# A graph network kernel: in each pass SP fetches some of the gathered rows, in place of the Pool's gather

## The reference

```python
h = relu(layernorm(x)); x = x + segment_sum(norm[:, None] * h[src], dst)      # norm from softmaxes of the edge weights
h = relu(layernorm(x)); for beta in betas (2): h = agnn_layer(h, src, dst, beta); x = x + h
h = relu(layernorm(x)); x = x + segment_sum(h[src] @ W16[type16], dst)        # 16 relations
h = relu(layernorm(x)); x = x + segment_sum(h[src] @ W32[type32], dst) / deg + h @ W_self + bias
```

## Time and profile before

| | |
|---|---|
| median of 3 runs | 12,770.65 us |
| profiled execution, its own time | 12,762.47 us |
| span of the profiled execution | 12,760.7 us |
| POOL busy | 9,421.5 us (74%) |
| PE busy | 7,159.6 us (56%) |
| DVE busy | 5,982.9 us (47%) |
| ACT busy | 2,502.0 us (20%) |
| granted TensorE clock | 0.503 of full speed |

### The profile page before, as it was taken

One profiled execution on the slowest core, in us unless ns is written; L12 is line 12 of the kernel. 1 busy time (PEld: TensorE's weight loads), 2 busy tenths in 40 slices (PEclk: granted clock), 3 DMA queues, 4 the chain that ended last, 5 costly groups with the idle time before them and its releaser, 6 DMA issues.

```text
span 12760.7 us, 121408 instructions
## 1 busy us (share of the span) xinstructions
PE 7159.6 (56%) x34866; PEld 5995.3 (47%) x34866; DVE 5982.9 (47%) x13186; ACT 2502.0 (20%) x5819; POOL 9421.5 (74%) x9933
## 2 busy tenths in 40 slices
PE   8430000444444688888878888875555554444444
PEld 2230000333333577777778888863333343333333
DVE  6991000333333587888778888862222222122221
ACT  0000000000000355555545555530000000000000
POOL 5777777777777677777767777767777776777777
PEclk5555555555555555555555555555555555555555
DMA  1001001111111222222222222232222222111112
GB/s 37 5 5 20 5 5 29 34 27 28 27 28 27 37 54 54 54 54 54 51 62 65 65 65 66 65 50 49 51 50 50 50 51 46 27 27 27 27 27 26
DMA packets 430148, 505.99 MB, mean 40 GB/s; under 512 B 235856, under 2 KB 245584, under 8 KB 417584
## 3 DMA queue, kind: packets, MB, share of 16 engines
q0 software_dynamic: 317504, 279.59, 14.5%
q1 hardware_dynamic: 97730, 214.09, 4.8%
q10 hardware_dynamic: 14316, 4.81, 0.2%
HBM read 397.49 MB, written 94.54 MB: 39 GB/s over the span
## 4 chain that ended last, share of the span: by engine, by line
POOL 68%; issue 23%; DVE 3%; PE 3%; DMA 2%; SPq 0%; DVEq 0%; ACT 0%; POOLq 0%; ACTq 0%
POOL Z L659 60%; POOL bins_dst L635 8%; DVE pd L1085 1%; DMA Z<-table,pd 1%; PE ps L1477 1%; PE ps L1479 1%; PE ps L1478 1%; DVE ps L1080 1%; PE ps L1558 0%; PE ps L1593 0%; DMA Z<-table_a,pd 0%; PE ps L1435 0%; PE ps L1524 0%; SPq L553 0%; DMA Z<-table_b,pd 0%
## 5 line engine op out<-in xcount | busy, mean ns | idle before, releaser
L659 POOL DMA_INDIRECT Z<-table,pd x4986 | 4704.8, 944 | 1623.0 <-issue 1513.6
L1575 PE MATMUL ps<-Z 128*128 128x65 f32 x9972 | 2326.7, 420 | 3334.5 <-DMA Z<-table_b,pd 1197.3
L1575 PEld LDWEIGHTS ps<-Z 128*128 128x128 f32 x9972 | 2186.3, 329 | 3654.2 <-issue 2348.2
L1131 DVE TENSOR_TENSOR Z<-ps,pd 128x768 f32<-128x768 f32 x831 | 795.0, 957 | 2836.8 <-PE ps L1575 2828.7
L635 POOL DMA_INDIRECT bins_dst<-slot_d x1612 | 1576.9, 978 | 589.7 <-issue 489.7
L659 POOL DMA_INDIRECT Z<-table_a,pd x1662 | 1568.3, 944 | 564.4 <-issue 560.6
L659 POOL DMA_INDIRECT Z<-table_b,pd x1662 | 1568.2, 944 | 545.0 <-issue 505.3
L1558 PE MATMUL ps<-Z 128*128 128x65 f32 x6648 | 1527.6, 417 | 268.8 <-DVE Z L1203 258.9
L1558 PEld LDWEIGHTS ps<-Z 128*128 128x128 f32 x6648 | 1467.2, 331 | 349.7 <-issue 216.9
L1524 PE MATMUL ps<-pay_d,hot 128*128 x6648 | 1554.8, 424 | 122.1 <-issue 97.4
L1524 PEld LDWEIGHTS ps<-pay_d,hot 128*128 128x128 f32 x6648 | 1463.7, 330 | 230.4 <-issue 227.8
(11 more groups left out here) (245 smaller groups left out, 8690.2 us busy)
## 6 DMA issues: line engine op xcount, KB each, us to landing
pay_d<-locals_ SPq DMA_DIRECT2D x92, 1152.0 KB
Z<-table,pd POOLq DMA_INDIRECT x4986, 2.4
table_b<-pay_d SPq DMA_DIRECT2D x192, 256.0 KB, 2.4
Z<-table_a,pd POOLq DMA_INDIRECT x1662, 2.4
Z<-table_b,pd POOLq DMA_INDIRECT x1662, 2.4
bins_dst<-slot_d POOLq DMA_INDIRECT x1612, 2.1
table_a<-kept SPq DMA_DIRECT2D x94, 256.0 KB
slot_d<-pay_d SPq DMA_DIRECT2D x62, 91.0 KB, 1.9
```

The source lines that it names most:

```text
L659: nc.gpsimd.indirect_dma_start(rows[:, at.slot, j, 0:width], None, ps_.table, bass.IndirectOffsetOnAxis(ap=pdi[:, g * ITEMS + j, ps_.colum ...
L1131: v.tensor_tensor(hot_d[:, at.three, :, :], every, nodes, ALU.is_equal).then_inc(hot_f_made, 1)
L1575: last = mm(p_pair[:, at.three, bass.ds(offset_of(at, j), ROW)], hot_d[:, at.three, j, :], given, start=False, stop=j == ITEMS - 1)
```

## The change

In five lists `TAKEN`, one for each pass, stand the groups 25, 37, 49, ... (in pass 2 from 30, in pass 3 from 28, in pass 4 from 21), every twelfth group up to 256: 20, 20, 19, 20 and 20 of them, 99 in all. Of these groups the Pool leaves out the last item, the sixth. SP fetches its 128 rows instead. It reads their numbers, which an own DMA has brought into `cand` or `node_max`, eight at a time into registers (one TENSOR_LOAD of 8 words), and issues for each row one DMA from the table to `fetched`, a new tensor in DRAM. 64 rows (`half_fetched`) stand behind the store of each block r = 0 to 39; behind the store of block r = 2t + 2 stands `into_ring`, which waits for the rows of the t-th fetched item and for the ring's place and moves them by one DMA into the ring. The consumers of these groups wait for this DMA as well (`ring_filled`). A row of 64 floats is split into 16 pieces of 4, a row of 65 floats (AGNN passes) into 13 pieces of 5. The chunks of `locals_` move ahead by one block.

```diff
+    FIRST = (25, 25, 30, 28, 21)
+    TAKEN = [range(first, NG - 20, 2 * RING) for first in FIRST]
+    fetched = scratch("fetched", (sum(len(t) for t in TAKEN), P, ROW))
...
+            def half_fetched(ps_, turn):
+                t, half = turn // 2, turn % 2
+                if t >= len(TAKEN[ps_.p]):
+                    return
...
+                for first in range(half * P // 2, (half + 1) * P // 2, BATCH):
+                    known = nc.values_load_multi_w_load_instructions(
+                        index_of[ps_.p % 2][t:t + 1, first:first + BATCH].bitcast(I32), engines=[sp.engine], min_val=0,
+                        max_val=ps_.table.shape[0] - 1, skip_runtime_bounds_check_because="rows of edges or the row of the padding")[1]
+                    for k in range(BATCH):
+                        sp.dma_start(fetched[n, first + k:first + k + 1, 0:width],
+                                     ps_.table[bass.ds(known[k], 1), :]).then_inc(row_fetched[n % 10], 16)
...
+            def into_ring(ps_, turn):
+                t = turn // 2 - 1
+                if turn % 2 or not 0 <= t < len(TAKEN[ps_.p]):
+                    return
...
+                sp.wait_ge(row_fetched[n % 10], (n // 10 + 1) * P * 16)
+                sp.wait_ge(msg_made if ps_.scaled else summed, done(at.g + (ps_.gather if ps_.scaled else ps_.every) - RING))
+                sp.dma_start(rows[:, at.slot, ITEMS - 1, 0:width], fetched[n, :, 0:width]).then_inc(ring_filled, 16)
...
             for r in range(NB):
                 store_rows(0, r)
+                into_ring(p_edge, r)
+                if r == 1:
+                    indices(p_agnn[0])
+                half_fetched(p_edge, r)
...
@@ gather @@
                         if j == ITEMS - 1 and ago:
-                            pool.wait_ge(gathered[ago.slot], (ps_.gathers(ago) + 1) * (16 * THREE))
+                            pool.wait_ge(gathered[ago.slot], landed(ps_, ago))
+                        if j == ITEMS - 1 and g in TAKEN[ps_.p]:
+                            continue
...
@@ multiply; the same in messages and sums_per_node @@
-                    dve.wait_ge(gathered[at.slot], (ps_.gathers(at) + 1) * (16 * THREE))
+                    dve.wait_ge(gathered[at.slot], landed(ps_, at))
+                    if at.g in TAKEN[ps_.p]:
+                        dve.wait_ge(ring_filled, ring_fills(ps_, at))
```

More of the change, by code:

```diff
@@ L357, in gnn_program @@
         local_loaded = [sem("local_loaded0"), sem("local_loaded1")]
+        indices_loaded = sem("indices_loaded")
+        row_fetched = [sem(f"row_fetched{k}") for k in range(10)]
+        ring_filled = sem("ring_filled")
         hot_t_made, hot_32_made, pen_made, fallen = sem("hot_t_made"), sem("hot_32_made"), sem("pen_made"), sem("fallen")
@@ L388, in gathers, with taken_before, landed, ring_fills @@
                 return self.nth * -(-(NG - at.slot) // RING) + at.rnd
+        def taken_before(ps_, at):
+            return sum(1 for q in range(ps_.p + 1) for g in TAKEN[q] if g % RING == at.slot and (q < ps_.p or g <= at.g))
+        def landed(ps_, at):
+            return (ps_.gathers(at) + 1) * (16 * THREE) - 16 * taken_before(ps_, at)
+        def ring_fills(ps_, at):
+            return 16 * (sum(len(TAKEN[q]) for q in range(ps_.p)) + TAKEN[ps_.p].index(at.g) + 1)
         p_edge = Pass(EDGE, 0, 0, 0, tables[0])
@@ new lines, in half_fetched @@
+            def half_fetched(ps_, turn):
+                t, half = turn // 2, turn % 2
+                if t >= len(TAKEN[ps_.p]):
+                    return
+                if turn == 0:
+                    sp.wait_ge(indices_loaded, 16 * (ps_.p + 1))
+                    if ps_.scaled:
+                        sp.wait_ge(table_stored, table_stores(ps_.p))
+                    else:
+                        for h in range(HALVES[ps_.p - 1]):
+                            sp.wait_ge(half_stored[h], 16 * NB * (ps_.p - 2 if h < HALVES[2] else 1) + 1)
+                n = sum(len(TAKEN[q]) for q in range(ps_.p)) + t
+                width = ROW if ps_.softmax else D
+                for first in range(half * P // 2, (half + 1) * P // 2, BATCH):
[5 more added lines that the diff above has]
+                                     ps_.table[bass.ds(known[k], 1), :]).then_inc(row_fetched[n % 10], 16)
@@ new lines, in into_ring @@
+            def into_ring(ps_, turn):
+                t = turn // 2 - 1
+                if turn % 2 or not 0 <= t < len(TAKEN[ps_.p]):
+                    return
+                at = At(TAKEN[ps_.p][t])
+                n = sum(len(TAKEN[q]) for q in range(ps_.p)) + t
+                width = ROW if ps_.softmax else D
+                sp.wait_ge(row_fetched[n % 10], (n // 10 + 1) * P * 16)
+                sp.wait_ge(msg_made if ps_.scaled else summed, done(at.g + (ps_.gather if ps_.scaled else ps_.every) - RING))
+                sp.dma_start(rows[:, at.slot, ITEMS - 1, 0:width], fetched[n, :, 0:width]).then_inc(ring_filled, 16)
@@ L575, in store_halves @@
                 for h in range(HALVES[p]):
+                    if h and chunk_between:
+                        chunk(*chunk_between)
                     sp.wait_ge(part_kept, part_of(p, rank, (h + 1) * 512 // WIDTH[p]))
@@ L591, in _ @@
                 store_rows(1, r)
[L592 to L597, removed]
+            for c in range(2, 4):
+                chunk(*chunk_of(2 * NG, c))
+            for r in range(NB):
+                store_halves(2, r, chunk_of(2 * NG, r + 4) if r + 4 < chunks else None)
+                into_ring(p_agnn[1], r)
+                if r == 1:
+                    indices(p_plain[0])
+                half_fetched(p_agnn[1], r)
             for r in range(NB):
                 store_halves(3, r)
+                into_ring(p_plain[0], r)
+                if r == 1:
+                    indices(p_plain[1])
+                half_fetched(p_plain[0], r)
             for r in range(NB):
@@ L1571, in sums_per_node @@
                         pe.wait_ge(half_gathered[at.slot], (ps_.gathers(at) + 1) * (16 * THREE))
-                        pe.wait_ge(gathered[at.slot], (ps_.gathers(at) + 1) * (16 * THREE))
+                        pe.wait_ge(gathered[at.slot], landed(ps_, at))
+                        if at.g in TAKEN[ps_.p]:
+                            pe.wait_ge(ring_filled, ring_fills(ps_, at))
                     for j in range(ITEMS):
```

32 lines of the change are left out of this document (26 added, 6 removed).

## The result

The changed kernel takes **15,573.83 us** (median of 4 runs, 15,567.83 to 15,581.91), the kernel before 12,771.22 us beside it (12,762.2 to 12,772.03): a ratio of 1.2194 with a 95% interval of 1.2179 to 1.221. The direction was forecast, the size was not: +2,803 us against +1,119, and outside the range.

The account below looks back on a forecast made before the run. The Pool's gathers bound the kernel; SP turns of 49.0 to 55.2 us, above 44.3, would add 1,126 us over the five passes, gathers saved included, to 12,762.5: 13,890 us on the median's scale, range 12,635 to 14,750.

Parts of the forecast that it names:

- the bound: All five passes: the Pool's gather sets the pace, 60% of the span, one start every 1.249 us.
- the saving: Pool: 99 gathers of 1.249 us removed, 123.6 us less; 12,647 us if all else keeps up.
- the mechanism: SP's queue: next store and fill wait behind 64 fetches, so too long turns delay the Pool; +1,126 us over five passes.
- the formula for a pass: Each pass: block 0's store plus 40 turns (38 in pass 2), landing and remaining gathers; pass 0 +115 us, pass 1 +348.
- Rows of 65 floats go out in 13 pieces.: SP's fetch in AGNN passes: 0.08 us more, 0.59 us each, 37.8 us for 64; bounds 0 and 0.11.
- Address and DMA 0.51 us.: SP's fetch of one row: 0.51 us with its address, 32.6 us for 64; bounds 0.43 to 0.66.
- Register loads of 8 words 1.8 us.: SP's row-number loads: 1.8 us each, eight with gaps 14.6 us a turn; other values 2.0, 1.2, lowest 0.27.
- The rule on increments: SP's DMAs on fewer than 16 engines: sequencer writes missing increments; if free, passes 1 and 2 lose some 400 us less.
- the fill in time: Ring, pass 0: with SP on time, a late fill costs no Pool time until some 44 us late.
- the DMA engines no limit: DMA engines: busy 17% to 26%; 12,672 more rows in small pieces add a few per cent.

Follow-up runs that it names:

- e14: Against the kernel before: the 99 items are neither gathered by the Pool nor fetched, their places keep old rows; 12,660.08 us, 0.9899.
- e9: Against the changed kernel: SP fetches each row as one piece into SBUF (unused columns of `iota`) and fills the ring from there; 12,635.74 us.
- e12: Against the changed kernel: SP still fetches all rows to DRAM, but the Pool gathers everything and nobody fills the ring; 15,281.06 us.
- e11: Against the changed kernel: AGNN passes fetch 80 floats in 16 pieces of 5 instead of 65 in 13; 13,950.81 us.
- e13: Against the changed kernel: 49 groups taken instead of 99, each fetched in four turns of 32 rows, still to DRAM; 12,693.45 us.
- e1: First run of the kernel that neither gathers nor fetches the 99 items, beside a slow kernel before; 15,578.67 against 15,699.22 us, 0.9917.
- e8: First run of the changed kernel with 49 groups, each fetched in four turns of 32 rows, beside a slow kernel before; 16,573.92 us, 1.0614.
- e5: First run of the changed kernel with empty SP loops in place of all fetches, the Pool gathering everything; 33,361.3 us, 2.1364.
- e10: Against the changed kernel: empty SP loops replace all fetches and their loads, the Pool gathers everything; 25,248.13 us, 1.9786.

## Why the prediction was right in its direction and wrong in its size

**Right: the bound, the saving, the mechanism.** The Pool's gathers were the bound and 99 of them are worth 124 us (e14: 130, e9: 126). SP can't leave a turn early, and the Pool's end follows SP's stores: the last gather starts 141 us after that of block 40 in pass 0 (4479.63 - 4338.26), where the working had 139 to the gather's end, and 158 in pass 1, where it had 152. So the formula for a pass holds, and nearly the whole error of 1,684 us (15,574 - 13,890) is in the turns put into it. One part was left out. The working named the fill as what frees the ring. The waits of DVE and ACT for the stores and chunks do nearly the same by themselves (e12), and the fill adds 290 us of 2,803.

**Wrong, and nearly three quarters of it: "Rows of 65 floats go out in 13 pieces."** The step took 0.08 us more for a fetch, with 0.11 as the upper bound from the two DMAs of L501. Measured: 0.758 instead of 0.492 us, +0.27, three times as much, and +0.5 us for each load behind it. That is 64 x 0.27 + 8 x 0.5 = 21 us a turn instead of 5. Turns of 54.7 and 55.2 us were forecast, 72.5 and 73.5 came. The forecast had put some 400 us on the 13 pieces; with them gone (e11) the kernel takes 13,951 us, 1,623 less. That is 1,220 of the 1,684 us. That 13,951 lies so near the 13,890 of the forecast is chance, for by the same working a kernel without the 13 pieces would take about 13,490; the other 460 us are the smaller errors below and in the rest of a turn. The bound failed because it rested on a single pair of DMAs from before the loops, which differ in rows as well as in pieces, and because a price for the instruction behind wasn't looked for.

**Wrong: "Address and DMA 0.51 us."** It was 0.675, beyond the upper bound of 0.66. The DMA alone took 0.492 and not 0.332. The nearest row by price was L517's 0.486, which I had kept only as an end of the range; I had reasoned by the number of engines, and the loads of x have that in common with a fetch too but cost a third less. 64 x 0.165 = 10.6 us a turn too little.

**Wrong: "Register loads of 8 words 1.8 us."** It was 0.53 us behind the cheaper DMAs. SP's load of one word takes 0.272, so seven more words cost 0.26 us together, 37 ns each, and not a round trip each. 8 x 1.27 = 10.2 us a turn too much. PE's 0.769 for three words didn't carry over to SP. The Trainium skill ("Runtime: NRT & Kernel Launch", section "Instruction fetch mechanics") gives about 200 ns for each register, in bulk too; these runs don't agree.

The last two cancel almost exactly, so that the edge and plain passes look well forecast: 49.0, 50.5 and 49.0 us said, 51.0, 53.9 and 51.1 found. Two errors of 10 us stand behind that, and another kernel would show them. In the sum, the turns give (2.0 + 17.8 + 3.4 + 2.1) x 40 + 18.3 x 38 = 1,707 us, against the 1,674 by which the passes are longer than forecast (2,800 - 1,126); the 33 us between them, in the starts and ends of the passes, aren't taken apart.

**The rule on increments.** By the Trainium skill ("DMA: Bandwidth & Descriptors", section "Why a DMA increments its semaphore by 16 and not by 1") a DMA on fewer than 16 engines makes the sequencer write the missing increments. The 13-piece DMAs agree in sign, with three missing: +0.27 us, and the load behind waits 0.5 us longer (e11 against after). But the one-piece DMAs of e9, with fifteen missing, cost 0.228 us, the least of all, and the load behind them 0.79 and not 0.53. So the missing increments can't be priced apiece, and whether the 0.27 us are theirs isn't shown.

**Right: the fill in time, the DMA engines no limit.** With SP on time, the fills cost nothing, from SBUF (e9) or from DRAM (e13). The fetches into DRAM made the gathers' packets slower, and in e13 no pass was longer by it.

**Open.** e9 changes two things at once, one piece instead of 16 and SBUF instead of DRAM as the destination; which of them makes the DMA cheap wasn't separated. Why a load of eight words takes 0.53, 0.79 or 1.04 us by the DMA ahead of it is measured, not explained. Whether the late store or the late chunk holds pass 1 wasn't separated either. What made instructions come late in e1 to e8 is unknown.

## What to carry to other kernels

Before work is given to an engine that "does next to nothing", count the turn it must keep (here 44.3 us) in instructions and ask what else stands in its queue: late stores and chunks cost 2,500 us here, with no more work than before on any compute engine. A DMA's issue is priced by its shape and destination, not as "a DMA": 0.23, 0.49 and 0.76 us for 256 to 260 bytes, which decided between 1% faster and 22% slower. When the price of a step that is repeated 12,672 times isn't in the trace, its bounds belong in the forecast as wide as the unlike rows make them, and a size that none of them shows (13 pieces between two DRAM buffers) deserves an end well beyond the nearest row.

## What the runs showed of the hardware that was not expected

- SP's issue of a DMA for one row: 0.228 us as one piece into SBUF, 0.492 us in 16 pieces from DRAM to DRAM, 0.758 us in 13. Fewer pieces is not cheaper in order, and 80 floats in place of 65 saved 1,623 us.
- A load of eight registers behind the 13-piece DMAs took 1.04 us, behind 16-piece ones 0.53, behind one-piece ones 0.79 (medians).
- Seven more registers in one load cost SP 0.26 us in all.
- A round of an empty loop with one satisfied wait took SP 0.25 us.
- The kernel before took 15.6 to 15.7 ms instead of 12.8 beside e1 to e8, on two chips. It isn't a fixed trait of the chip: e5 to e8 and e10 to e13 have the same chip number, and beside the latter, 25 minutes later, it took 12,761 us. In e1, the left-out kernel's DVE shows waits of this kind (us in total, times, longest):

```profile
DVE Z L1218 <- remote: 3797.8, 300, 32.8
```
